# Neighbour sum: the block transpose of a batch's values moved from TensorE and ScalarE to a second load and VectorE

## What is computed

```
idx = _knn(x_loc, k)                         # 30 neighbours of each of the 1024 points
...
att = jax.nn.softmax(h[..., 0], axis=-1)
xk = x.transpose(0, 2, 1)[bidx, idx]
agg = jnp.einsum('bnkc,bnk->bnc', xk, att)
return x + agg.transpose(0, 2, 1)
...
out = _chunk_attn(q, k, v, masks, ...) + x
mu = jnp.mean(out, axis=2, keepdims=True)
return (out - mu) * jax.lax.rsqrt(var + EPS)
```

## Time and profile before

| | us |
|---|---|
| median of 3 runs | 6317.76 |
| lowest, highest | 6315.41, 6318.28 |
| profiled execution, its own time | 6316.55 |
| its span | 6314.8 |
| TensorE busy | 5517.6 (87%) |
| VectorE busy | 5699.2 (90%) |
| ScalarE busy | 4499.4 (71%) |
| GpSimd busy | 3397.5 (54%) |
| mean granted TensorE clock | 0.935 |

### The profile page before, as it was taken

How to read it: one execution, slowest core, us unless ns; L and a number is a source line. 1 busy time by engine, 2 the same in 40 slices (tenths; PEclk the granted TensorE clock), 3 DMA queues, 4 the chain that set the end, 5 groups by cost and what they waited for, 6 DMA issues and landing times. The chain is left out here.

```text
span 6314.8 us, 227176 instructions
## 1 busy us (share of the span) xinstructions
PE 5517.6 (87%) x82516; PEld 3384.3 (54%) x82516; DVE 5699.2 (90%) x8045; ACT 4499.4 (71%) x17145; POOL 3397.5 (54%) x3375
## 2 busy tenths in 40 slices
PE   7888888888888888888888888888669859999999
PEld 3555555555555555555555555555433347777776
DVE  7999999999999999999999999999855687777786
ACT  7888888888888888888888888888604623333333
POOL 3466666666666666666666666666620033333332
PEclk9999999999999999999999999999879979999999
DMA  2333333333333333333333333333340023333332
GB/s 45 95 105 97 99 98 96 95 95 107 98 110 91 99 98 96 97 97 109 96 107 93 97 97 97 97 108 92 106 108 0 0 64 89 94 87 88 84 94 74
DMA packets 651349, 568.72 MB, mean 90 GB/s; under 512 B 553072, under 2 KB 574832, under 8 KB 616208
## 3 DMA queue, kind: packets, MB, share of 16 engines
q1 hardware_dynamic: 613264, 284.51, 19.2%
q10 hardware_dynamic: 36864, 268.45, 12.0%
HBM read 384.76 MB, written 67.24 MB: 72 GB/s over the span
## 5 line engine op out<-in xcount | busy, mean ns | idle before, releaser
L722 ACT ACTIVATE prob<-SC,row_max 128x64 f32<-128x64 f32 x6144 | 1842.2, 337 | 389.7 <-DVE row_max L1046 381.6
L835 POOL TENSOR_TENSOR prob<-prob,row_rec 128x512 f32<-128x512 f32 x768 | 830.2, 1082 | 1433.5 <-DVE row_rec L1054 1403.5
L722 ACT ACTIVATION_READ_ACCUMULATOR prob<-SC,row_max 128x1 f32 x6144 | 1393.0, 230 | 0.0
L1038 DVE FIND_INDEX8 nbr<-top,dist 128x8 uint16<-128x1024 f32 x1024 | 1234.4, 1217 | 0.0
L1031 DVE MAX8 top<-dist 128x8 f32<-128x1024 f32 x1024 | 1190.8, 1203 | 1.7
L1033 DVE MATCH_REPLACE8 dist<-top,dist 128x1024 f32<-128x1024 f32 x768 | 923.3, 1206 | 0.0
L586 PE MATMUL SC<-k_bd,q_t 128*64 128x256 f32 x6144 | 907.1, 420 | 0.0
L1697 ACT ACTIVATE dense<-DM 128x512 f32<-128x512 f32 x512 | 305.6, 597 | 747.0 <-PE DM L1656 746.7
L607 PEld LDWEIGHTS PT<-ident,prob 128*128 128x128 f32 x3072 | 361.7, 145 | 833.8 <-issue 815.6
L1805 DVE TENSOR_TENSOR d_oh_a<-lo,iota_a 128x4096 bf16<-128x4096 bf16 x256 | 583.9, 2291 | 239.7 <-PE DM L1656 239.1
L607 PE MATMUL PT<-ident,prob 128*128 128x128 f32 x3072 | 490.9, 284 | 351.0 <-ACT prob_t L729 350.3
(11 more groups left out here) (187 smaller groups left out, 9475.7 us busy)
## 6 DMA issues: line engine op xcount, KB each, us to landing
low_all<-low_scratch ACTq DMA_DIRECT2D x256, 1024.0 KB, 5.0
k_bd<-k_t SPq DMA_DIRECT2D x3072, 16.0 KB, 1.9
placed<-compact SPq DMA_DIRECT2D x256, 192.0 KB, 3.8
ctx<-in_ctx SPq DMA_DIRECT2D x32, 512.0 KB, 6.2
mask<-in_mask SPq DMA_DIRECT2D x32, 512.0 KB, 8.7
xb<-in_x SPq DMA_DIRECT2D x32, 512.0 KB, 3.3
x_scratch<-xb SPq DMA_DIRECT2D x32, 512.0 KB, 6.9
y_scratch<-y_b SPq DMA_DIRECT2D x32, 512.0 KB, 6.6
```

The lines of the kernel that those rows point to most:

```text
L722: last = act.activation(prob[:, s % 4, g * CHUNK:(g + 1) * CHUNK], SC[:, s % 2, g * CHUNK:(g + 1) * CHUNK], ACT.Exp, bias=row_max[:, s % 2 ...
L835: pool.tensor_tensor(pr, pr, row_rec[:, r % 2, :].unsqueeze(2).to_broadcast([128, 8, CHUNK]), ALU.mult).then_inc(normed, 1)
L1038: last = dve.max_index(nbr[:, uu % BPB, t, k * 8:(k + 1) * 8], best, row)
```

## The change

The eight transposes on TensorE, the copy on ScalarE, the identity tile and the PSUM tile `XT` go. In their place the batch's values are loaded a second time, into a tile `x2_q`, with the 32x32 blocks already at the place that they have in the transposed matrix: 16 transfers a batch, each to 32 partitions, 8 pieces of 32 floats in a row (32 KB). VectorE then turns every 32x32 block with one transpose of 128x1024 (`turn_quarters`), after `weights` at t=3. SP issues the 16 transfers at the head of its body, ahead of `nb` and `placed` h=1, once the transpose of the batch before has read the tile. The first 16 stand ahead of all `placed`, and the first `turn_quarters` ahead of the first `weights`.

```
-        ident = sb("d_ident", [128, 128])
+        x2_q = sb("x2_q", [128, T])
-        XT = ps("XT", [128, 2, 512])
...
+            def by_quarters(batch):
+                rows = dram["x2"][batch].rearrange("(w c) (t q m) -> q c t w m", w=4, q=4, m=32)
+                for q in range(4):
+                    dst = x2_q[32 * q:32 * q + 32, :].rearrange("c (t w m) -> c t w m", w=4, m=32)
+                    for w in range(4):
+                        sp.dma_start(dst[:, :, w, :], rows[q][:, :, w, :]).then_inc(quarters_in, 16)
...
 (SP body)
                 b = counter(i, u)
+                if not is_last(i, u):
+                    sp.wait_ge(xt_ready, START + b(1, 1))
+                    sp.sem_inc(passed, 1)
+                    by_quarters(b(1, 1))
...
-                        sp.wait_ge(xt_ready, START + before(1, 1))
-                        sp.sem_inc(passed, 1)
                         sp.wait_ge(xy_ready, START + before(1, 1))
...
+            by_quarters(0)
             spread_blocks(0, 0, 0)
...
 (TensorE)
-                    pe.wait_ge(xt_copied, START + b(1, 1))
+                    pe.wait_ge(xt_ready, START + b(1, 1))
...
-                pe.wait_ge(x2_in[u], START + (i + 1) * 16)
-                pe.wait_ge(xt_copied, START + b(1))
-                for t in range(NT):
-                    last = pe.transpose(XT[:, t // 4, (t % 4) * 128:(t % 4 + 1) * 128], x2[:, u, t * 128:(t + 1) * 128], ident[:, :])
-                last.then_inc(xt_ready, 1)
...
 (ScalarE)
-                act.wait_ge(xt_ready, START + b(1, 1))
-                if not is_first(i, u):
-                    act.wait_ge(summed, START + b(2, -1))
-                act.activation(x2_t[:, u, :, :].rearrange("p t c -> p (t c)"), flat(XT[:, :, :]), ACT.Identity).then_inc(xt_copied, 1)
...
 (VectorE)
+            def turn_quarters(b, u, read_before):
+                dve.wait_ge(quarters_in, START + b(256, 256))
+                if read_before is not None:
+                    dve.wait_ge(summed, START + read_before)
+                dve.sem_inc(passed, 1)
+                dve.transpose(x2_t[:, u, :, :].rearrange("p t c -> p (t c)"), x2_q[:, :]).then_inc(xt_ready, 1)
...
                     if t == 3 and not is_last(i, u):
                         weights(counter(i, u + 1))
+                        turn_quarters(counter(i, u + 1), (u + 1) % BPD, None if is_first(i, u) else b(2))
...
             indices(counter(0, 0), 0, 0)
+            turn_quarters(counter(0, 0), 0, None)
             weights(counter(0, 0))
```

More of the change, by code:

```diff
@@ L1527, in neighbour_sum @@
         dense_copied = sem("dense_copied")
+        quarters_in = sem("quarters_in")
         xt_ready = sem("xt_ready")
-        xt_copied = sem("xt_copied")
         summed = sem("summed")
@@ L1540, in neighbour_sum @@
         passed = sem("d_passed")
-        CONSTS = [(ident[:, :], "ident"), (iota[:, :], "iota_a"), (iota_m[:, :], "iota_m"), (minus_half[:, :], "pow_half")]
+        CONSTS = [(iota[:, :], "iota_a"), (iota_m[:, :], "iota_m"), (minus_half[:, :], "pow_half")]
         block = es.enter_context(nc.Block())
```

## The result

The changed kernel takes 6412.93 us (median of 4 runs, 6402.2 to 6420.22) where the kernel before takes 6316.59 beside it (6311.62 to 6318.28): 1.0152 times as long, 95% interval 1.0135 to 1.017. The forecast was 6350, its range ended at 6385: the sign was right, the size was not. The profiled execution took 6408.88.

A forecast was written before the change was run, and what follows sets the result against it. TensorE and VectorE were taken to end within about a microsecond in u=1, with TensorE's transposes on the path in u=0. Start + 11.6, turns - 12.6, waits + 34.5 gave + 33.5 on 6316.55: 6350, range for 8 in 10 6308 to 6385.

The forecast's parts named there:

- The issues on SP and the wait at part 4: u=1 batches: 16 issues at 0.80 us outrun the 10.7 us slack of `placed` h=1; TensorE waits 2.3 us, 34.5 lost.
- The wait at part 4 drops the clock: Rival, chance 0.10: the 2.3 us wait lowers the clock, next `AG` loses 1.15 us in each of 15; 6367.
- Removed in u=1: Head of u=1: removing 1.33 us of TensorE transposes gains nothing, since VectorE delivers part 0's spread only at 5594.85.
- Removed in u=0: Behind the turn: removed transposes save 0.9 us (bounds 0.6 to 1.76), 14 times, 12.6 us gained.
- No wait in u=0: u=0 batches: `placed` has 15.2 us of slack, more than the 13.0 us delay, so TensorE does not wait.
- The start: Start of the stage: first `weights` transpose 6.9 us later, part 4 waits 4.7; 11.6 us lost, bounds 5 and 14.
- VectorE: New transpose per batch takes 1.2 us; spread of part 4 ends 0.6 us late alongside the 2.3 us wait, adding nothing.
- The engines can't carry the pieces: Rival, chance 0.10: at twice 31.6 ns a packet, part 4's spread comes 4 us late and `placed` 5; 6391.

The follow-up runs named there:

- the last version: Kernel before, with second load and VectorE transpose only for u=0 batches, loads in SP's idle time, 16 padding instructions ahead of the loop: 6307.77 us (0.9983).

## Why the prediction was right in sign and wrong in size

- **The issues on SP and the wait at part 4** (15 x 2.3 = 34.5 us). The mechanism was right, and so were the pace (0.84 us for 0.80) and the delay of `placed` (12.9 us for 13.0). The size was not, and the agreement of 34.3 us with 34.5 is luck: only 24.5 us of it are at part 4 of u=1, in 10 waits and not 15, because in the other batches the head of u=1 had already lost the time. Where it loses nothing, the wait is 3.6 to 3.8 us on average, above the forecast's upper bound of 3.4, since TensorE then reaches part 4 about 1 us sooner than the slack of 10.7 us allowed for.
- **The clock behind that wait.** "The wait at part 4 drops the clock" was a rival with 0.10, at 1.15 us each. It is what happens: part 4 to the next turn takes 0.94 us more in the pair shown and 1.06 on average, the `AG` 4.74 us.
- **Removed in u=1: "worth nothing"**. This step failed. VectorE does deliver last, and TensorE does wait (0.8 to 1.4 us in the batches shown, by the `placed` of h=0 or by VectorE). I asked what hides the transposes and not what the gap does once they are gone. It is mostly followed by clock 0.50 and costs 1.5 us per batch where the loop lies well (7.48 for 5.94 from part 0 to part 1), shown by putting the transposes back. In the kernel after, the head of u=1 costs 1.66 us per batch, some 22 us that the forecast had at nothing; in five of its batches a pause near the end of part 0 adds to it, whose cause is open.
- **Removed in u=0: 14 x 0.9 = 12.6 us gained.** This step failed most. The work removed is worth 1.6 to 1.7 us per turn if the loop lies well, near the upper bound of 1.76 and not 0.9. But the step took the turn as the 4.29 us that it was the earlier trace rows; the removed instructions moved the loop across a block edge and the turn got a second pause of 2.1 to 2.6 us, so turn to part 1 went from 8.20 to 9.23. The term came out at + 14 us (13 x 1.06) for - 12.6. Without loads the block alone is worth 61 us, with them 22. (The fourteenth gap of the earlier trace rows is no turn but the way into the loop, 1.32 us; the loop goes back 13 times.)
- **No wait in u=0.** Nearly right for `placed` (0.5 us in one wait), but the small pauses in parts 2 to 4 weren't foreseen: 0.40 us per batch, and with the `AG` behind them 0.55 more from part 1 to the next part 0.
- **The start** (6.9 + 4.7 = 11.6 us): 5.0 to the first `DM` and 3.7 at part 4, so 8.7, within its bounds of 5 and 14. The queue and the order were right.
- **VectorE** (1.2 us, no slack behind it): 1.245, and it waits 27.4 us for `x_q` in all, alongside TensorE's wait at part 4.
- **"The engines can't carry the pieces"**: refuted. It had `placed` 5 us late in each u=1 batch by the traffic alone; issued at another place, the same transfers cost 5 us in the whole run.

Put together by the runs: the removal with the loop well placed and no loads in it, about 21 us gained at the turns (13 x 1.6) and 20 lost at the heads of u=1 (13 x 1.5), 7 lost at the start, 6324.5 measured; the loads at the head of SP's body, 67 more, 6391; the block edge, 22 more, 6413. So the predicted term for the loads was the largest of them, and it was half of what they cost (34.5 for 67): the wait was 3.7 us and not 2.3, a slower clock followed it (0.9), and u=0 lost 1.2 us where nothing had been expected, less 1.4 us at the head of u=1. That is 4.4 us in each of the 12 periods from the first turn to the last, 52 us; the rest is lost ahead of them and behind.

Open is what makes the clock rise earlier in one turn and later in another, and with that why the last version gained 10 us and not 24.

## What to carry to other kernels

Removing or adding instructions in or ahead of a loop moves the loop on the instruction blocks: compare the packets of the instruction queue before and after, and if there is about one more per turn, move the loop with a few empty instructions before judging the change. Work that fills a gap on TensorE may be worth keeping, since what the gap does to the clock falls on the large matmuls behind it. A batch of small transfers is priced by the queue that issues it and by what stands behind it, so it belongs where that queue has nothing urgent to come.

## What the runs showed of the hardware

- The granted clock fell to 0.50 behind pauses of only 0.82 to 1.40 us at the head of u=1, with busy stretches of small matmuls ahead of them; the eight fp32 `AG` then take 4.95 to 5.18 us for 3.68. In the two versions without transposes, with the loop well placed and without loads at the head, 25 of the 26 u=1 batches behind a turn are like that (pauses of 0.98 to 1.83 us, `AG` 4.93 to 5.30). It isn't so every time: in the run with 1 KB pieces a pause of 1.25 us left the `AG` at 3.68, and in the run without second load four of 13 left them at 3.7 to 4.0. What decides it is open.
- Where the first block edge is near behind the turn of a loop, TensorE goes on 4.1 to 4.2 us after the turn's own pause ended, whether 7 or 15 matmuls or the transposes were done till then (5583.58 - 5579.46 and 5658.29 - 5654.05; 5579.80 - 5575.73 in the run without second load); over all turns of these runs it is 3.8 to 4.5 us. That is about the length of the turn's pause again, so the second block seems to be asked for only when the first is there; that is an inference. With the loads issued at the head it was 3.2 us (5600.31 - 5597.09; 2.9 on average, with 1 KB pieces too), behind `placed` h=1 again 4.0; why it is shorter with them at the head is open.
- Sixteen transfers of the same bytes are issued in 8.5 to 11.6 us where their pieces are 1 KB and the destination has no gaps, and in 11.7 to 14.1 us in 128-byte pieces with gaps.
- A VectorE transpose of 128x1024 in fp32 takes 1245 ns, in line with 0.45 us for 256 elements and 692 ns for 512.
